# Three small edits to an attention and mixture-of-experts layer: where a wait for zero fills stands, where the first step's transposes stand, and how a batch's total is counted

## The reference

```python
# attention, x: (8, 512, 128)
xn = layernorm(x)
kv = (xn @ w_kv_down) @ w_kv_up             # 128 -> 128 -> 2048
q  = xn @ w_q                               # 128 -> 1024
att = softmax(causal(q . k / 8))            # 16 heads of 64
x  = x + (att . v) @ w_out
# experts
flat = layernorm(x).reshape(-1, 128)
top_vals, top_idx = top_k(flat @ Wr, 2)     # 8 experts
combine = softmax(top_vals) put at top_idx
h  = silu(flat @ Wg[e]) * (flat @ Wu[e])    # 128 -> 512
out = x + sum_e combine[e] * (h @ Wd[e]) * 12 ** -0.5
```

## Time and profile before

| what | value |
|---|---|
| runs shown | 877.3, 879.77 and 880.31 us, median 879.77 us |
| the profiled execution, its time | 877.01 us |
| its span, first to last instruction | 875.1 us |
| busy share of the span | PE 97%, PEld 77%, ACT 72%, DVE 71%, POOL 65% |
| attention steps | about 28 to 665 us, one in 9.8 us |
| experts | about 665 to 865 us, the last scatters to 869 us |

### The profile page before, as it was taken

How to read it: one execution, slowest core, us unless ns; L and a number is a source line. 1 busy time by engine, 2 the same in 40 slices (tenths; PEclk the granted TensorE clock), 3 DMA queues, 4 the chain that set the end, 5 groups by cost and what they waited for, 6 DMA issues and landing times. The chain is left out here.

```text
span 875.1 us, 20176 instructions
## 1 busy us (share of the span) xinstructions
PE 848.5 (97%) x6559; PEld 672.4 (77%) x6559; DVE 620.8 (71%) x2348; ACT 625.8 (72%) x1639; POOL 572.4 (65%) x522
## 2 busy tenths in 40 slices
PE   7999989999999999999999999999999999999995
PEld 4677767777777777777777777777777999988884
DVE  5677767878787877777787878878887665544442
ACT  5777767887777778777887778787786776555452
POOL 5375548468756856794688578667757667555565
PEclk9999999999999999999999999999999999999998
DMA  7484550000000000000000000000011334333343
GB/s 195 196 291 196 237 169 1 2 13 19 8 1 31 3 7 8 25 5 4 13 20 7 1 29 4 8 7 25 6 29 44 47 57 65 45 49 48 46 54 28
DMA packets 44039, 44.71 MB, mean 51 GB/s; under 512 B 4112, under 2 KB 36240, under 8 KB 43936
## 3 DMA queue, kind: packets, MB, share of 16 engines
q0 software_dynamic: 16528, 26.03, 12.4%
q1 hardware_dynamic: 27120, 17.25, 7.2%
q10 hardware_dynamic: 288, 0.13, 0.1%
HBM read 15.28 MB, written 28.12 MB: 50 GB/s over the span
## 5 line engine op out<-in xcount | busy, mean ns | idle before, releaser
L407 POOL TENSOR_TENSOR prob<-prob,row_inv 128x512 f32<-128x512 f32 (+3 forms) x256 | 318.6, 1264 | 207.1 <-DVE row_inv L851 199.7
L585 ACT ACTIVATE prob<-prob,neg_max 128x256 f32<-128x256 f32 (+3 forms) x512 | 280.5, 550 | 7.6 <-DVE neg_max L844 0.9
L1318 PE MATMUL low_ps<-PT,v_sb 128*64 128x512 f32 (+3 forms) x1024 | 152.0, 439 | 0.3 <-ACT PT L591 0.3
L1318 PEld LDWEIGHTS low_ps<-PT,v_sb 128*64 128x64 f32 x1024 | 68.1, 136 | 92.1 <-issue 65.2
L856 DVE COPY PT<-low_ps 128x512 f32<-128x512 f32 (+1 forms) x128 | 104.2, 814 | 23.5 <-PE low_ps L1305 21.1
L596 ACT ACTIVATE v_sb<-mid_ps 128x512 f32<-128x512 f32 x64 | 38.2, 598 | 93.8 <-PE mid_ps L1242 93.6
L1156 DVE TENSOR_TENSOR prob<-mid_ps,prob 128x512 f32<-128x512 f32 x71 | 49.0, 691 | 77.9 <-PE mid_ps L1242 40.1
L1305 PE MATMUL low_ps<-ident,prob 128*128 128x128 f32 x640 | 94.9, 279 | 6.2 <-POOL prob L407 3.8
L844 DVE CUSTOM_DVE_ANT_0 prob<-mid_ps,mask 128x128 f32<-128x128 f32 (+1 forms) x256 | 93.5, 421 | 9.2 <-PE mid_ps L1291 5.0
L585 ACT ACTIVATION_READ_ACCUMULATOR prob<-prob,neg_max 128x1 f32 x512 | 95.7, 187 | 0.0
L591 ACT ACTIVATE PT<-top_ps 128x1024 f32<-128x1024 f32 x64 | 65.7, 1026 | 38.1 <-PE top_ps L1305 32.7
(11 more groups left out here) (257 smaller groups left out, 1878.7 us busy)
## 6 DMA issues: line engine op xcount, KB each, us to landing
routed_rows<-W_dn POOLq DMA_DIRECT2D x8, 2080.0 KB
X<-routed_rows SPq DMA_DIRECT2D x37, 65.0 KB
X<-routed_rows SPq DMA_DIRECT2D x17, 130.0 KB
X<-in_L_attn_x SPq DMA_DIRECT2D x8, 256.0 KB, 5.5
W_ffn<-in_L_ffn_Wg SPq DMA_DIRECT2D x8, 256.0 KB, 4.9
W_ffn<-in_L_ffn_Wu SPq DMA_DIRECT2D x8, 256.0 KB, 5.1
W_dn<-in_L_ffn_Wd SPq DMA_DIRECT2D x8, 256.0 KB, 4.6
out<-X SPq DMA_DIRECT2D x8, 256.0 KB, 2.3
```

Source lines behind the costliest of these rows:

```text
L407: nc.gpsimd.tensor_tensor(p_pair(i), p_pair(i), row_inv[:, i, :].unsqueeze(2).to_broadcast([P, 2, P * (i + 1)]), ALU.mult).then_inc(S["nor ...
L585: nc.scalar.activation(p_at(i, h), p_at(i, h), ACT.Exp, bias=neg_max[:, i, h:h + 1], scale=-1.0, accum_out=row_sum[:, i, h:h + 1]).then_in ...
L1318: last = nc.tensor.matmul(y_ps[h * HD:(h + 1) * HD, j * P:T], v_sb[:, half, j, o + h * HD:o + (h + 1) * HD], PT[:, h, j, j:NT, :].rearrang ...
```

## The change

Three edits. First, POOL's wait for the fills is moved from the end of step 8 to just ahead of the first row scatter. Second, in the first step PE does the transposes of row tile 1 ahead of the fold v1, those of tile 2 behind it, those of tile 3 between the second and the third value chunk, and those of tile 0 behind the fourth; DVE's copy of tile 1 and ACT's copy of tile 3 move with them. Third, `post_ranks` gets the total from the products for the ranks, which are made one tile wider, so that the four products for the total alone go.

```diff
-RANK_COL, TOTAL_COL = 64, 128
+RANK_COL = 64
+TOTAL_COL = RANK_COL + NT * E
...
             def post_scatter(b, first, end):
...
+                if b == 0 and first == 0:
+
+                    pool.wait_ge(S["rows_written"], 16 * (FILLS + 1))
                 for k, t in [(k, t) for k in range(K) for t in range(NT)][first:end]:
...
             fill_last()
-            pool.wait_ge(S["rows_written"], 16 * (FILLS + 1))
             for m in range(1, B - 1):
...
             for bank, t in step0:
                 v_copy(t, 0, t, bank)
+            t3_copy(0)
             act.wait_ge(S["kv_ready"], 4)
             w_hi(Wk, 1, post_ps[:, :])
-            t3_copy(0)
...
             w_lo(Wv, 0, 3, post_ps[:, :])
+            t_copy(0, 1)
             inv(0, 3)
             qk_lo(1)
             w_lo(Wv, 1, 4, post_ps[:, :])
-            for i in (1, 2, 0):
+            for i in (2, 0):
                 t_copy(0, i)
...
-                ranks = post_bank(b)[:, RANK_COL:RANK_COL + NT * E].rearrange("p (t e) -> p t e", e=E)
-                total = post_bank(b)[:, TOTAL_COL:TOTAL_COL + E]
+                ranks = post_bank(b)[:, RANK_COL:RANK_COL + (NT + 1) * E].rearrange("p (t e) -> p t e", e=E)
                 kw = dict(skip_group_check=True)
-                nc.tensor.matmul(ranks, before_bf[:, :], chosen_bf[:, :, :], start=True, stop=True, **kw)
-                for t in range(NT - 1):
-                    nc.tensor.matmul(ranks[:, t + 1:NT, :], ones_bf[:, :],
-                                     chosen_bf[:, t:t + 1, :].to_broadcast([P, NT - 1 - t, E]), start=False, stop=True, **kw)
+                nc.tensor.matmul(ranks[:, 0:NT, :], before_bf[:, :], chosen_bf[:, :, :], start=True, stop=True, **kw)
+
                 for t in range(NT):
-                    last = nc.tensor.matmul(total, ones_bf[:, :], chosen_bf[:, t, :], start=False, stop=True, **kw)
+                    last = nc.tensor.matmul(ranks[:, t + 1:NT + 1, :], ones_bf[:, :],
+                                            chosen_bf[:, t:t + 1, :].to_broadcast([P, NT - t, E]), start=False, stop=True, **kw)
...
             project(1, 1, 0)
+            transposes(0, 1)
             pe.wait_ge(S["wlo_done"], 3)
             fold("v1", post_ps[:, :], 3 * T)
+            transposes(0, 2)
             for t in range(NT):
...
                 v_chunk(t, 0, 0, t, t % 2)
-            for i in (1, 2, 0):
-                transposes(0, i)
+                if t == 1:
+                    transposes(0, 3)
+            transposes(0, 0)
             pe.wait_ge(S["wlo_done"], 4)
             fold("k1", post_ps[:, :], T)
-            transposes(0, 3)
```

## The result

The changed kernel takes 869.65 us (868.56 to 870.71, four runs) against 879.59 us before: 9.9 us less, ratio 0.9892, 95% interval 0.9873 to 0.9911. Two later measurements of the same change gave 0.9896 (0.9880 to 0.9911) and 0.9891 (0.9875 to 0.9907). The forecast was 7.0 us, which is a ratio of 0.992: the right direction and inside the range, but 2 to 3 us short, just outside all three intervals. The profiled execution took 868.56 us, its span is 866.8 us.

The account below looks back on a forecast made before the run. The prediction took PE's own work to bound the kernel, busy for 97% of the span. Its terms, 5.0 + 1.4 + 0.6 = 7.0 us, taken from the 879.8 us median, gave 872.8 us, range 869.0 to 876.5 us.

Parts of the forecast that it names:

- the 0.8 us of POOL at tile 3: PE's wait for POOL's normalised probabilities at tile 3, 0.8 us, placed around step 9 behind the fills' wait.
- the wait for ACT's copy of the fourth chunk: First step: new PE wait ahead of tile 0's transposes, which use that chunk's bank; 0.9 us.
- The slack of DVE's copy: First step: DVE's copy of tile 1 has 0.4 us to spare before tile 2; at worst 0.7 us lost.
- The check by idle times: First step: of 2.67 us PE idle time about 1.5 us are left, which makes a gain of 1.2 us.
- The row: Profile row for the ranks' matmuls: eight take 0.21 us, 26 ns each, so 24 fewer win 0.6 us.
- the 81 ns: The Trainium skill's price for a narrow matmul with its weight load in a stream; by it 1.9 us won.
- The sum: Whole kernel: 5.0 + 1.4 + 0.6 = 7.0 us won, carried to the end.
- a rival on the slow side: Experts' end: scatters' landings queue up under the shifted schedule and the kernel ends slower, 882.4 us; chance 0.03.
- The clock's fall in the first step: First step: short transposes among gaps drop PE's clock to half, costing 1.7 us, time 874.5 us; chance 0.04.
- Slower landings: Experts' end: six scatters' landings would take 9.6 us more to end 0.3% slower, 882.4 us; chance 0.03.

Follow-up runs that it names:

- step0_only: The kernel before with only the first step's new order on PE, DVE and ACT: 874.8 us, ratio 0.9980 to the kernel before.
- warm_wait: The kernel before with 16 idle matmuls on PE in step 9, where it waits for POOL and the fills: 875.3 us, one run.
- fold_first: The changed kernel with the fold k1 ahead of the transposes of tile 0 in the first step: 868.7 us, ratio 0.9911 to the kernel before.
- fold_again: The changed kernel with the fold k1 ahead of tile 0's transposes, measured a second time unchanged: 868.6 us, ratio 0.9883 to the kernel before.
- pe_order_only: The kernel before with PE's new order in the first step, but DVE's and ACT's copies left in the old order: 878.7 us, one run.
- wait_only: The kernel before with only POOL's wait for the fills moved: 871.6 us, ratio 0.9943 to the kernel before.

## Why the prediction came out as it did

**Edit 1** was right in place and size: 14.83 - 9.77 = 5.06 us for a forecast of 5.00, POOL released within 0.1 us, no new wait at the first scatter, no slower normalisation under the fills in flight (1.04 us for the first of step 9, as for that of step 15). Two of its sentences were wrong, though neither changed the sum. It put the 0.8 us of POOL at tile 3 into step 9; that wait is in step 62, the last but one of the attention, and is in both traces. And it treated the fall of the clock as a fixed part of the stall. The runs show that it is the uncertain part: among the traces with the wait, PE idled for 3.42 to 4.39 us, and what the step took above 9.78 and that idle time was 1.4 to 1.6 us in the five in which the clock fell (14.70 to 15.69 us for the step) and nothing in step0_only. warm_wait shows the two apart in one place. The wait's price was therefore 3.7 to 5.9 us from one trace to the next, which the prediction gave as one number. The step distance was still the right reading of that one trace.

**Edit 2** came out at 1.42 us for 1.4, by its own steps: the fold kept its place, tile 2 went in at 19.28, the chunks began 0.2 us earlier only because the execution did, and the wait for ACT's copy of the fourth chunk was 0.78 us for 0.9. The slack of DVE's copy held. The check by idle times (1.2 us) was the worse figure.

**Edit 3**: 0.07 us a step for 0.08, in six of the seven steps; about 0.5 us for 0.6. The row was the better price than the 81 ns.

**The sum** is where it failed. PE's side came out as forecast: DVE's last instruction is 865.38 - 858.05 = 7.33 us earlier, of which 0.20 are the start, so 7.1 for 7.0: 5.1 in step 9, 1.4 in the first step, 0.4 in the steps from 10 on, the rest in the experts, where traces of one kernel differ by as much. That 7.1 and 7.0 agree to 0.1 us is partly luck. What failed is the sentence that idle time closed "is carried to the end as long as PE stays the engine that is waited for". At the end of the kernel before it was not: the earlier trace rows and the page's chain showed that already, and the prediction used them only for a rival on the slow side. The last scatter started 2.26 us behind DVE in the first trace of before and 1.23 us in that of the change. This 1.03 us more makes the 8.4 us by which the two spans differ. Over the traces, this lag is 2.3 to 5.0 us in seven that lack one edit or more (mean 3.7) and 1.2 to 3.0 in five that have all three (mean 1.8); the traces with late idle matmuls are left out of both. The difference of 1.9 us is about the size of what the timed gain has over 7.0 (2.1 to 2.9 us by the medians), but it is a comparison made afterwards over traces of several kernels.

**What stays open** is why. The backlog is worked off by some 50 scatters, each of which may wait 3 to 4 us for a landing, and single landings took up to 2 us longer at different slots in different traces. That explains lags that jump about, and fold_first (3.01) against fold_again (1.23) shows chance of that size in one and the same kernel. It doesn't explain that the change should have the smaller ones on average; with five and seven traces whose lags overlap chance isn't excluded, while three timed comparisons of 9.1 to 9.9 us speak against it.

There is a second candidate that the traces can't settle: clock falls in executions that weren't traced. The mean granted clock of the timed executions is 0.996 or 0.997 for the changed kernel, 0.990 to 0.995 for the kernel before, and the time goes with it (877.2 and 877.3 us at 0.995, 879.3 to 881.5 at 0.990 in the last group). One fall as in step 9 takes 0.002 off the mean. The two traces of the kernel before have 0.995 and 0.993, so its executions at 0.990 had more half clock than either: another fall, as in the first step of pe_order_only, or a longer idle end. In wait_only, which keeps the old first step, the mean goes from 0.997 (869.8 us) down to 0.992 (874.9 us) with no wait in step 9 at all. If it is a further fall, part of the surplus is PE's after all. No run here tells a cause.

**Rivals.** The clock's fall in the first step didn't happen in the change and did in pe_order_only, behind an idle time of 2.65 us: the fall is real, and the Trainium skill's rule (TensorE: Matmul & The Clock Gate, section Part 4: PE-mode transpose) that transposes don't count as busy in the same way still can't be told from plain idling by it; in the change the clock stays at 1.00 through all twenty. Slower landings were given 3% as a loss; they are no rival to the edits but a part of every run, 1.2 to 5.0 us from DVE's last instruction to the last scatter.

## What to carry to other kernels

Price a stall by the distance of like steps, but ask separately whether the clock fell behind it: that part came in five of six traces here. Moving a wait is free if its new place has cover, and worth more than PE's idle time where the clock fell behind it. Before carrying a gain "to the end", read what the last instruction waited for: where a chain of DMA landings ends the span, the time is the later of two sums, and a gain on one of them arrives with an error as large as the other one's scatter.

## What was not expected of the hardware

With idle times of 3.42 to 4.39 us the granted clock fell to 0.50, for about 3.4 us each time, in five traces, but with 3.67 us in step0_only it stayed at 1.00, and with 2.65 us in the first step of pe_order_only it fell, over a microsecond after PE had gone on. The length of the idle time alone doesn't tell which.

From the last scatter's start to the end of the span it was 7.5 us in all fourteen traces, while the distances between scatters in the backlog ranged from 1.9 to 5.9 us.
